# Layer 0 of a two-layer state-space kernel: where ScalarE copies the raw step projection out of PSUM

## What is computed

```
x_dbl = einsum('bkdl,kcd->bkcl', xs, x_proj_weight)
dts, Bsx, Csx = split(x_dbl, [R, R + N], axis=2)          # R = 12, N = 16
dts = einsum('bkrl,kdr->bkdl', dts, dt_projs_weight)
delta = softplus(dts + dt_projs_bias)
dA = exp(delta * A);  h = dA * h + (delta * u) * B;  y = einsum('bkdn,bkn->bkd', h, C)
```

## Time and profile before

| | us |
|---|---|
| median of 3 runs | 17118.56 (17107.04 to 17120.23) |
| profiled execution, its time | 17104.75 |
| its span, first to last instruction | 17103.0 |
| DVE busy | 15041.9 (88%) |
| POOL busy | 13820.5 (81%) |
| PE busy (modelled ends) | 13081.6 (76%) |
| ACT busy | 8696.2 (51%) |
| mean granted clock of PE | 0.912 of full speed |

### The profile page before, as it was taken

How to read it: one execution, slowest core, us unless ns; L and a number is a source line. 1 busy time by engine, 2 the same in 40 slices (tenths; PEclk the granted TensorE clock), 3 DMA queues, 4 the chain that set the end, 5 groups by cost and what they waited for, 6 DMA issues and landing times.

```text
span 17103.0 us, 102091 instructions
## 1 busy us (share of the span) xinstructions
PE 13081.6 (76%) x29328; PEld 5263.8 (31%) x29328; DVE 15041.9 (88%) x9070; ACT 8696.2 (51%) x7907; POOL 13820.5 (81%) x5869
## 2 busy tenths in 40 slices
PE   7777777777777787777877778777777777777777
PEld 2322333323333233322333323332233332333323
DVE  8998889988899888998889988899888998889988
ACT  4445744457444574445744456444574445644456
POOL 7987779877798777987779877798777987779877
PEclk9998989989899998999989989899898998989989
DMA  5552245522455224552255522555225552255522
GB/s 171 194 182 93 74 169 195 181 95 74 172 194 180 94 74 170 195 182 93 74 172 194 182 94 73 172 193 182 93 73 176 192 182 92 73 175 191 182 91 73
DMA packets 688754, 2442.01 MB, mean 143 GB/s; under 512 B 78396, under 2 KB 100168, under 8 KB 688200
## 3 DMA queue, kind: packets, MB, share of 16 engines
q1 hardware_dynamic: 688200, 2435.49, 41.1%
HBM read 2419.45 MB, written 15.73 MB: 142 GB/s over the span
## 4 chain that ended last, share of the span: by engine, by line
PE 31%; DVE 25%; POOL 18%; issue 17%; DMA 5%; ACT 3%; DVEq 0%; SPq 0%; POOLq 0%; ACTq 0%
PE bank L465 14%; POOL room L778 13%; DVE room L936 8%; DVE room L928 8%; DMA room<-bc_rows 5%; DVE room L998 4%; PE bank L474 4%; PE bank L419 4%; PE bank L341 3%; DVE room L1018 3%; POOL room L787 3%; PE bank L499 2%; PE bank L396 2%; PE bank L385 2%; POOL room L753 1%
## 5 line engine op out<-in xcount | busy, mean ns | idle before, releaser
L928 DVE TENSOR_TENSOR_SCAN room<-bank,room 128x1024 f32<-128x1024 f32 x3072 | 6954.7, 2278 | 551.8 <-ACT bank L594 551.5
L778 POOL TENSOR_TENSOR room<-room 128x1024 f32<-128x1024 f32 x3072 | 7167.1, 2365 | 262.6 <-DMA room<-bc_rows 208.6
L419 PE MATMUL bank<-room,identity 128*128 128x512 f32 x12288 | 6266.9, 638 | 499.1 <-DVE room L936 324.1
L594 ACT ACTIVATE bank<-room,a 128x1024 f32<-128x1024 f32 x3072 | 3412.4, 1116 | 4295.4 <-DVE room L928 4282.5
L465 PE MATMUL bank<-room,identity 128*128 128x512 f32 x6144 | 3128.1, 657 | 1046.4 <-DVE room L1018 895.8
L998 DVE TENSOR_TENSOR_SCAN room<-bank,room 128x1024 f32<-128x1024 f32 x1536 | 3438.5, 2274 | 59.4 <-POOL room L825 45.1
L419 PEld LDWEIGHTS bank<-room,identity 128*128 128x128 f32 x12288 | 2439.8, 203 | 3204.0 <-issue 2304.2
L936 DVE TENSOR_TENSOR room<-room,bank 128x1024 f32<-128x1024 f32 x2360 | 2822.2, 1196 | 284.3 <-PE bank L406 279.2
L406 PE MATMUL bank<-parts,pick_row 96*128 96x512 bf16 x4720 | 1488.8, 398 | 1695.7 <-DVE room L936 1638.3
L825 POOL TENSOR_TENSOR room<-room 128x1024 f32<-128x1024 f32 x768 | 2301.3, 3019 | 30.1
L787 POOL TENSOR_TENSOR room<-room 128x1024 f32<-128x1024 f32 x712 | 1678.4, 2357 | 740.0 <-DVE room L928 740.0
(11 more groups left out here) (88 smaller groups left out, 9344.4 us busy)
## 6 DMA issues: line engine op xcount, KB each, us to landing
room<-bc_rows SPq DMA_DIRECT2D x4552, 512.0 KB, 4.4
wx<-in_w_x SPq DMA_DIRECT2D x65, 162.0 KB
bc_rows<-xdbl SPq DMA_DIRECT2D x72, 128.0 KB, 4.2
xT<-in_x SPq DMA_DIRECT2D x8, 768.0 KB, 5.7
out_x<-xT SPq DMA_DIRECT2D x8, 768.0 KB, 4.3
win<-in_w_in SPq DMA_DIRECT2D x16, 288.0 KB, 3.2
room<-in_w_in SPq DMA_DIRECT2D x16, 288.0 KB, 5.4
room<-in_w_out SPq DMA_DIRECT2D x16, 288.0 KB, 5.8
```

The costliest lines, as they stand in the source:

```text
L419: ins = nc.tensor.matmul(bank[:, YACC + h, :], identity[:, :], state0[:, g % STATES, halves(h)], start=(n == 0), stop=(n == N - 1))
L594: nc.scalar.activation(whole(DECAY0[g % 2]), delta0[:, j, :], ACT.Exp, scale=a0[:, col:col + 1]).then_inc(S["decay"], note("decay", (i, j, ...
L778: nc.gpsimd.tensor_tensor(source0[:, g % SOURCES, :], du0[:, j, :], b_ring0[:, g % BROWS, :], ALU.mult).then_inc(S["source"], note("source ...
L928: nc.vector.tensor_tensor_scan(run(state0[:, g % STATES, :]), run(whole(DECAY0[g % 2])), run(source0[:, g % SOURCES, :]), 0.0, ALU.mult, A ...
```

## The change

```diff
@@ ACT, scans0, in the loop over g
                             first_part(b, p[1])
                     elif p and p[0] == "z":
                         take(b, ("z", 0, p[2], p[3]), gate[0][:, p[2], halves(p[3])], p[3])
-                    p = piece(g - 1)
-                    if p and p[0] == "dt":
+                    elif p:
                         take_dt(b, p[1], p[2])
```

## The result

The changed kernel takes 16867.46 us (median of 4 runs, 16856.75 to 16879.64) against 17112.8 (median of 4, 17105.59 to 17120.23) beside it: ratio 0.9857, 95% interval 0.984 to 0.9874. That is 245 us less; I had forecast 16905 with a range of 16815 to 16990. The profiled execution took 16879.64 us, the slowest of the four, and the profiled one of the kernel before 17104.75, so between the two traces 225 us are to be explained. Lines behind L616 stand one number lower than in the kernel before.

The account below looks back on a forecast made before the run. DVE was taken to bound layer 0, waiting 551.5 us for ACT's decay behind a copy. Gains of 218 us over eight images, less 8 for POOL's lead, gave 210: forecast 16905 us, range 16815 to 16990.

Follow-up runs that it names:

- e10: Changed kernel, with PE adding the state of unit 2 right behind the spread of unit 3 instead of behind that of 6: 16790.75 us, ratio 0.9809.
- e11: e10 with PE's sum of unit 4 also issued behind the spread of unit 6: 16666.83 us, ratio 0.9735.
- e12: e11 with SP's weight load moved from the pass with j = 0 to the one with j = 1: 16675.87 us, ratio 0.9741.
- e13: e11 with the copy at its old place, as in the kernel before: 17011.34 us, ratio 0.9938.
- e9: Changed kernel with SUM_LAG 5 instead of 4, so PE adds states weighed by POOL one unit later: 17247.08 us, ratio 1.0074.
- e7: Changed kernel with PE's sum of unit 4 issued behind the spread of unit 6, and SUM_LAG 5 instead of 4: 17161.75 us, ratio 1.0023.

## What to carry to other kernels

When an engine that works in order waits for another's result in front of something that is ready, put the ready thing first, and count what then is late: here half of the gain came back at the next user of the same two banks. Read that bound from the producer's list (projection, sum, spread) and not from the copy. An order that loses alone can win beside another: the spread ahead of the sum cost 65 us with two sums behind it and gave 124 with one. Look for real work to put in the gap ahead of a burst before making room behind it.

## What I had not expected of the hardware

A sum of 1.9 us moved into PE's gap of 3.1 us behind the spread of 3 took away every projection that is slow from end to end: 0 of 120 in e10, e11, e12 and e13, against 47 before, 38 in the changed kernel and 23 or more in every run without it. Partly slow ones are left, 23, 18, 14 and 34. Pass (1, 1) of the kernel before (spread of 4 behind the gap, then the sum of 3) and the same place in e10:

```profile
307.68 0.89 PE L406 MATMUL bank<-parts,pick_row 96*128 96x512 bf16 x2 [3.11 <-DVE room L936]
...
308.36 3.32 PE L419 MATMUL bank<-room,identity 128*128 128x512 f32 x4
```

```profile
297.27 0.59 PE L406 MATMUL bank<-parts,pick_row 96*128 96x512 bf16 x2 [1.38 <-DVE room L937]
297.70 1.88 PE L419 MATMUL bank<-room,identity 128*128 128x512 f32 x4
```

Behind 3.11 us of idle time the sum takes 3.32 us, behind 1.38 it takes 1.88. It is the place in the gap that does it, and not the absence of that sum behind the spread of 6: e9 and e7 take it away from there too, put it later, and have 41 and 23 slow projections. Whether it is the shorter gap or the work in it, no run here tells apart.

PE's half-speed stretches (1.2 GHz) did not become fewer by much for it: the mean granted clock of e11 is 0.922 against 0.912 before and 0.924 in the changed kernel. They lie elsewhere now, as behind the spread in the timeline of e11, where the sum takes 3.26 us, and there less waits for them. So the share of time at half speed says little; which burst it meets is what counts.
